# Expert layers: down projection with activations as the stationary operand, residual stream kept in rows of tokens

## What is computed

```python
x = x + tanh(g_xattn[1]) * L1_xattn_ref(ctx, ctx, layernorm(x), ssm_kernel, D, 8)   # long convolution
x = x + tanh(g_ffn[1])  * L1_ffn_ref(layernorm(x), ...)                             # experts
# L1_xattn_ref: kv = k (x) v; y = causal convolution of kv with ssm_kernel, + kv * D; out = sum of y * q
# L1_ffn_ref:
gate = xf @ Wg + bg                       # router, 6 of 8 kept, softmax
h  = silu(xf @ Wgate + bgate) * (xf @ Wup + bup)      # per expert, hidden 256
eo = h @ Wdown + bdown
share = silu(xf @ Ws_up + bs_up) @ Ws_down + bs_down
out = sum_n eo[n] * w[n] + share
```

## Time and profile before

| | before |
|---|---|
| median of three runs | 2029.07 us (2028.69 to 2031.53) |
| profiled execution, its own time | 2031.29 us |
| its span, first to last instruction | 2029.5 us |
| mean granted TensorE clock over the span | 0.975 |
| TensorE matmul busy | 95% of the span |
| VectorE, ScalarE, GpSimd busy | 73%, 51%, 51% |
| start of `experts_block` | at about 659 us |

### The profile page before, as it was taken

How to read it: one execution, slowest core, us unless ns; L and a number is a source line. 1 busy time by engine, 2 the same in 40 slices (tenths; PEclk the granted TensorE clock), 3 DMA queues, 4 the chain that set the end, 5 groups by cost and what they waited for, 6 DMA issues and landing times.

```text
span 2029.5 us, 27663 instructions
## 1 busy us (share of the span) xinstructions
PE 1920.4 (95%) x10020; PEld 1565.7 (77%) x10050; DVE 1484.9 (73%) x2229; ACT 1027.9 (51%) x1468; POOL 1037.0 (51%) x788
## 2 busy tenths in 40 slices
PE   6999769999997669999999999999999999999998
PEld 5888746666653658888888888888888888888886
DVE  5877569888884777867876976876886787687422
ACT  4447547776764435336337427335434633733532
POOL 1110144444430856665666665666565566576554
PEclk9999889999999779999999999999999999999999
DMA  5866415566645113324244233242332423421422
GB/s 196 312 239 230 180 47 136 145 164 172 148 112 131 62 33 129 95 84 147 72 120 131 73 119 107 96 126 79 130 105 87 142 70 112 146 78 63 135 99 68
DMA packets 170115, 249.72 MB, mean 123 GB/s; under 512 B 91356, under 2 KB 92764, under 8 KB 163708
## 3 DMA queue, kind: packets, MB, share of 16 engines
q1 hardware_dynamic: 169692, 247.86, 39.7%
q10 hardware_dynamic: 288, 0.10, 0.0%
HBM read 193.13 MB, written 33.69 MB: 112 GB/s over the span
## 4 chain that ended last, share of the span: by engine, by line
PE 61%; POOL 2%; DVE 1%; issue 1%; DMA 1%; SPq 0%; DVEq 0%; ACT 0%; POOLq 0%; ACTq 0%
PE e_ps_u L54 6%; PE e_ps_out L54 6%; PE e_ps_u L55 6%; PE e_ps_u L56 6%; PE e_ps_out L56 6%; PE e_ps_out L55 6%; PE e_ps_g L55 4%; PE e_ps_g L56 4%; PE e_ps_g L54 4%; PE e_ps_m L56 4%; PE e_ps_m L55 4%; PE e_ps_m L54 4%; PE e_ps_m L2873 1%; DMA e_dn_raw<-in_md 1%; PE e_ps_m L2827 1%
## 5 line engine op out<-in xcount | busy, mean ns | idle before, releaser
L1418 POOL TENSOR_TENSOR e_gu_lo<-e_gu_raw,e_gu_hi 128x1024 fp32r<-128x1024 f32 (+1 forms) x128 | 287.8, 2251 | 176.0 <-ACT e_gu_hi L1722 175.5
L2277 DVE TENSOR_REDUCE e_x3T<-e_zp 128x128 f32<-128x1024 f32 x124 | 256.6, 2070 | 6.4 <-ACT x_held L1837 5.3
L1423 POOL TENSOR_TENSOR e_dn_lo<-e_dn_raw,e_dn_hi 128x512 fp32r<-128x512 f32 x128 | 183.8, 1438 | 110.2 <-ACT e_dn_hi L1728 109.4
L54 PE MATMUL e_ps_u<-e_xn_hi,e_gu_hi 128*128 128x512 f32 x512 | 203.3, 397 | 0.0
L54 PE MATMUL e_ps_out<-e_hd_hi,e_dn_hi 128*128 128x512 f32 x512 | 201.8, 394 | 0.0
L55 PE MATMUL e_ps_u<-e_xn_lo,e_gu_hi 128*128 128x512 f32 x512 | 199.9, 390 | 0.0
L56 PE MATMUL e_ps_u<-e_xn_hi,e_gu_lo 128*128 128x512 f32 x512 | 199.8, 390 | 0.0
L56 PE MATMUL e_ps_out<-e_hd_hi,e_dn_lo 128*128 128x512 f32 x512 | 199.6, 390 | 0.0
L55 PE MATMUL e_ps_out<-e_hd_lo,e_dn_hi 128*128 128x512 f32 x512 | 199.5, 390 | 0.0
L2209 DVE TENSOR_TENSOR e_hd_lo<-gate_held,e_hd_hi 128x512 fp32r<-128x512 f32 x128 | 146.6, 1145 | 70.2 <-ACT e_hd_hi L1752 70.0
L1439 POOL TENSOR_TENSOR e_kv_raw<-e_ke 128x512 f32<-128x512 f32 x128 | 148.2, 1158 | 82.5 <-DVE e_kv_lo L2241 76.9
(11 more groups left out here) (316 smaller groups left out, 5070.3 us busy)
## 6 DMA issues: line engine op xcount, KB each, us to landing
e_gu_raw<-in_mgu SPq DMA_DIRECT2D x96, 512.0 KB, 3.8
e_dn_raw<-in_md SPq DMA_DIRECT2D x128, 256.0 KB, 2.8
e_wb<-wts SPq DMA_DIRECT2D x8, 1536.0 KB, 7.2
c<-in_ctxT SPq DMA_DIRECT2D x8, 1024.0 KB, 7.7
raw_w<-in_w1T SPq DMA_DIRECT2D x8, 1024.0 KB, 4.9
x_held<-in_w2T SPq DMA_DIRECT2D x8, 1024.0 KB, 7.4
gates<-gate_held SPq DMA_DIRECT2D x8, 1024.0 KB, 5.6
vals<-o SPq DMA_DIRECT2D x8, 1024.0 KB, 4.9
```

What stands on the lines that cost most here:

```text
L54: nc.tensor.matmul(out, w_hi, x_hi, start=first, stop=False, skip_group_check=skip)
L1418: nc.gpsimd.tensor_tensor(gu_lo[:, s % 2, a], gu_raw[:, s % 2, a], f32(gu_hi[:, s % 2, a]), ALU.subtract).then_inc(gulo_done, 1)
L1423: nc.gpsimd.tensor_tensor(dn_lo[:, s % 2], dn_raw[:, s % 2], f32(dn_hi[:, s % 2]), ALU.subtract).then_inc(dnlo_done, 1)
L2277: nc.vector.tensor_reduce(x3T[:, lb].rearrange("p (b n) -> p b n", b=B)[:, :, hh * CD:(hh + 1) * CD], zv(5, (1, 8), (21, 8)), AX.X, ALU.ad ...
```

## The change

The operands of the down projection change places: the stationary one is now a block of 128 tokens of `hd_hi` or `hd_lo`, the moving one the 512 columns of the down weights. So `ps_out` has tokens on partitions, like `x`. The matmul with the experts' biases (`bias`) is turned in the same way, and the shared bias becomes a further row of it, with weight one.

- `x2T`, `turn_x2`, `read_x2T`, `y`, `copy_x3` and the scaled bias `gb` go.
- `turn_x3` now turns the bare convolution result. Its wait for `add_x2` becomes a wait for the last `add_terms`; its second group waits for `add_x3(q, 0)` instead of for `norm_nat(q, 0)`.
- `add_x2` becomes `add_x3(q, a)`: two instructions of 1024 columns a tile, which read the turned result from PSUM and add into the rows of `x` in place. They stand ahead of `nat_stats(q, a)`. `nat_stats` and `norm_nat` read those rows from SBUF.
- `finish(g, j)` reads `ps_out` and adds into the same rows, for one block of 128 tokens each. `down_done` counts four times in a tile's last step, so that `finish(g, 0)` can begin when the first bank is done.
- `store` writes four transfers of 256 KB, each after its own `finish`.
- The tiles of `x` rotate over three buffers, `o`, `x_next` (new) and `x_held`. `load_x(q)` waits from the fourth tile on for the stores of tile q-3 and no longer for `norm_x` and `read_x2T`.
- GpSimd sets two more small constants at the start.

```diff
+    xs = [keep["o"], sb("x_next", [P, TJ, D]), keep["x2"]]
...
         def load_x(q):
-            sp.wait_ge(xq_done, START + 4 * q)
-            sp.wait_ge(x2T_done, START + 2 * q)
             sp.wait_ge(keep["x2_out"], START + 16 * TJ * NCH)
+            if q >= len(xs):
+                sp.wait_ge(y_out, START + 16 * TJ * (q - len(xs) + 1))
...
         def store(g):
-            sp.wait_ge(y_done, START + 4 * g + 4)
-            sp.dma_start(dram["out"].rearrange("g (k p) n -> g p k n", p=P)[g], y[:]).then_inc(y_out, 16)
+            for j in range(TJ):
+                sp.wait_ge(y_done, START + TJ * g + j + 1)
+                sp.dma_start(row_block(dram["out"], g, j), rows_of(g)[:, j]).then_inc(y_out, 16)
...
-        def add_x2(q, lb=None):
-            if lb is None:
-                dve.wait_ge(red_done, START + sums(CHD * KT * (q + 1)))
-                dve.wait_ge(x2T_done, START + 2 * (q + 1))
-                rows = slice(0, KT)
...
-            nc.vector.scalar_tensor_tensor(out=x3T[:, rows], in0=x3T[:, rows], scalar=keep["gains"][:, 1:2], in1=x2T[:, rows],
+        def add_x3(q, a):
+
+            dve.wait_ge(nat_filled, 2 * q + a + 1)
+            rows = rows_of(q)[:, 2 * a:2 * a + 2]
+            nc.vector.scalar_tensor_tensor(out=rows, in0=area(q, 1 + a), scalar=keep["gains"][:, 1:2], in1=rows,
                                            op0=ALU.mult, op1=ALU.add).then_inc(x3_done, 1)
...
             n = STEPS * g + s
             pe.wait_ge(hdlo_done, START + n + 1)
             pe.wait_ge(dnlo_done, START + n + 1)
-            for k in range(KT):
-                col = slice(k * P, (k + 1) * P)
-                last = products(nc, ps_out[:, k], dn_hi[:, s % 2, col], dn_lo[:, s % 2, col], hd_hi[:, s % 2], hd_lo[:, s % 2], False,
+            for j in range(TJ):
+                tok = slice(j * P, (j + 1) * P)
+                last = products(nc, ps_out[:, j], hd_hi[:, s % 2, tok], hd_lo[:, s % 2, tok], dn_hi[:, s % 2], dn_lo[:, s % 2], False,
                                 s == STEPS - 1, skip=True)
-            last.then_inc(down_done, 1)
-
-        def turn_x2(q, a):
-            pe.wait_ge(x_in, 16 * TJ * (q + 1))
...
+                if s == STEPS - 1 or j == TJ - 1:
+                    last.then_inc(down_done, 1)
...
         def turn_x3(q, a):
-            pe.wait_ge(x3_done, x3_count(q))
-            if a == 0:
-                pe.wait_ge(prod_done, START + 4 * CHD * KT * (q + 1))
-            elif q > 0:
-                pe.wait_ge(xnat_done, START + 4 * q + 2)
+            pe.wait_ge(red_done, START + sums(CHD * KT * (q + 1)))
+            if q == 0:
+                pe.wait_ge(pool_step, SETUP + 3 * len(SPLIT))
+            elif a == 1:
+                pe.wait_ge(x3_done, START + 2 * q + 1)
```

More of the change, by code:

```diff
@@ L1175, in experts_block @@
     RT = 15
+    SETUP = 4
     def view(t, offset, *dims):
@@ L1210, in toep_slot, with rows_of, downs @@
         return (t_lo if low else t_hi)[:]
-    def x3_count(q):
-        return START + (q + KT if q >= 0 else 0)
+    def rows_of(q):
+        return xs[q % len(xs)]
+    def downs(n):
+        g, s = divmod(max(n, 0), STEPS)
+        return START + (STEPS + TJ - 1) * g + s
     def at(op, c, *which):
@@ L1828, in cut_wT @@
             nc.scalar.activation(wT[:], ps_g[0:WROWS], ACT.Copy).then_inc(wThi_done, 1)
[L1830 to L1839 removed]
+        for s in (silu_done, xq_done, ke_done, qe_done, xnat_done):
             act.sem_inc(s, START)
@@ L1845, in setup @@
             nc.scalar.activation(wr[:, :, 0:8], wr_raw, ACT.Copy).then_inc(setup_hi, 1)
-        read_x2T(0, 0)
         setup()
@@ L1856, in _ @@
         read_q(0, 1)
-        read_x2T(0, 1)
         cut_dn(0, 0)
@@ L1875, in _ @@
         keys(1, 0)
-        copy_x3(0, 0)
-        copy_x3(0, 1)
         cut_kv(1, 0)
-        copy_x3(0, 2)
         cut_dn(0, 1)
@@ L1890, in _ @@
         cut_kv(1, 1)
-        copy_x3(0, 3)
-        read_x2T(1, 0)
         cut_gu(0, 2)
@@ L1895, in _ @@
         silu(0, 1)
-        read_x2T(1, 1)
         cut_hd(0, 1)
@@ L1985, in _ @@
         norm_x(2)
-        read_x2T(2, 0)
         cut_kv(2, 0)
@@ L1992, in _ @@
         read_lgT(1)
-        read_x2T(2, 1)
         cut_dn(1, 1)
@@ L2009, in _ @@
         cut_wT(1)
-        for k in range(4):
-            copy_x3(1, k)
         silu(1, 3)
@@ L2089, in _ @@
             at(norm_x, i + 1)
-            at(read_x2T, i + 1, 0)
             at(cut_kv, i + 1, 0)
@@ L2096, in _ @@
             at(read_lgT, i)
-            at(read_x2T, i + 1, 1)
             at(cut_dn, i, 1)
@@ L2113, in _ @@
             at(cut_wT, i)
-            for k in range(4):
-                at(copy_x3, i, k)
             at(silu, i, 3)
@@ L2410, in _ @@
         add_terms(0, 12)
-        add_x2(0, 0)
         multiply(0, 14)
@@ L2414, in _ @@
         multiply(0, 15)
-        add_x2(0, 1)
-        add_x2(0, 2)
         add_terms(0, 15)
-        add_x2(0, 3)
+        add_x3(0, 0)
         nat_stats(0, 0)
+        add_x3(0, 1)
         nat_stats(0, 1)
@@ L2507, in _ @@
         add_terms(1, 15)
-        add_x2(1)
         cut_hd(0, 12)
         gated(0, 13)
+        add_x3(1, 0)
         nat_stats(1, 0)
@@ L2514, in _ @@
         cut_hd(0, 13)
+        add_x3(1, 1)
         nat_stats(1, 1)
@@ L2607, in _ @@
         add_terms(2, 15)
-        add_x2(2)
+        add_x3(2, 0)
         nat_stats(2, 0)
@@ L2614, in _ @@
         cut_hd(1, 13)
+        add_x3(2, 1)
         nat_stats(2, 1)
@@ L2708, in _ @@
             at(add_terms, i + 1, 15)
-            at(add_x2, i + 1)
+            at(add_x3, i + 1, 0)
             at(nat_stats, i + 1, 0)
@@ L2715, in _ @@
             at(cut_hd, i, 13)
+            at(add_x3, i + 1, 1)
             at(nat_stats, i + 1, 1)
@@ L2775, in bias, with down_first @@
             if g == 0:
-                pe.wait_ge(setup_lo, 3)
+                pe.wait_ge(setup_lo, 2)
                 pe.wait_ge(setup_hi, 2)
             pe.wait_ge(wT_done, START + g + 1)
-            for k in range(KT):
-                last = nc.tensor.matmul(ps_out[:, k], bd[:, k * P:(k + 1) * P], wT[:], start=False, stop=False, skip_group_check=True)
+            for j in range(TJ):
+                last = nc.tensor.matmul(ps_out[:, j], wT[:, j * P:(j + 1) * P], bd[:], start=False, stop=False, skip_group_check=True)
             last.then_inc(bias_done, 1)
-        def down_first(g, k):
-            if k == 0:
+        def down_first(g, j):
+            if j == 0:
                 pe.wait_ge(hdlo_done, START + STEPS * g + 1)
@@ L2914, in _ @@
         up(0, 0)
-        turn_x2(1, 0)
         turn_lg(0)
         up(0, 1)
-        turn_x2(1, 1)
         for k in range(3):
@@ L2986, in _ @@
         down(0, 15)
-        turn_x2(2, 0)
         up(1, 0)
         logits(1)
-        turn_x2(2, 1)
         up(1, 1)
```

125 lines of the change are left out of this document (45 added, 80 removed).

## The result

The changed kernel takes 2034.72 us (median of nine executions, 2033.92 to 2036.29) against 2029.07 us of the kernel before (nine executions of it, 2026.66 to 2031.53). The ratio is 1.0029, with a 95% interval of 1.002 to 1.0038: 5.7 us or 0.3% slower, where 18.1 us faster was predicted. The span of its profiled execution is 2033.3 us, against 2029.5.

What follows compares the result with a forecast made beforehand. TensorE was taken to bound the long stretch, with other engines setting the time at both ends. Savings of 12.2 + 0.9 + 1.0 + 4.0 = 18.1 us from 2029.07 gave 2011.0 us, range 2006 to 2020.

Steps and rivals of the forecast that it cites:

- TensorE bounds the long stretch.: From 757 to 2022 us only TensorE's work sets the end; it is busy 1264.04 of 1265.00 us.
- 12.2 us for 14 groups: Removing `turn_x2`'s groups of eight transposes in the long stretch saves 0.87 us each, 12.2 us in all.
- The exchange of operands costs nothing: Down projection matmuls with weights as the moving operand keep 0.23 us from start to start: 0 us.
- rival 3: The 1536 down matmuls get slower with exchanged operands; at 20 ns each the time is 2041.7 us; chance 0.04.
- 0.9 us for the wait of `turn_x3`: TensorE's one wait, `turn_x3` behind `add_x2` in the long stretch, goes: 0.9 us saved.
- 1.0 us in the first tile: On VectorE's path in the first tile the last statistics come 1.0 us earlier; bounds 0 and 2.3.
- rival 4: Moved idle times in the first tile shift TensorE's granted clock; two 4 us stretches give 2015 us; chance 0.08.
- So the cover holds and I take 0: Where tiles meet, VectorE's two new additions fit within margins of 0.94 and 1.06 us, so TensorE loses 0.
- Rival 1: VectorE becomes the bound where two tiles meet, price up to 6.5 us, giving 2017.5 us; chance 0.10.
- 1.37 us of slack against 1.3: 0: SyncE's queue absorbs three more store issues a tile, 1.3 us, before the next expert weight load: cost 0.
- Its store of 256 KB lands in 2.3 to 2.9 us, as such stores do: At the kernel's end the last, smaller store lands sooner, so the span ends 4.0 us earlier, at 2025.5.
- the upper bound of the groups: Most that removing `turn_x2`'s 14 groups could save on TensorE: the full 1.03 us each, 14.4 us.

Runs made afterwards that it cites:

- experiment 6: Kernel of experiment 3 with the 14 groups of eight transposes put back as dead work that nobody reads: 2024.39 us, ratio 0.9976 to the kernel before.
- experiment 1: Changed kernel with the output laid out tile by tile, so each store is a plain 128x512 piece: 2021.04 us, ratio 0.9955 to the kernel before.
- experiment 11: Kernel of experiment 3 with early `x` loads in twelve 32x512 DMAs and GpSimd waiting for `nat_shift`: 2007.42 us, ratio 0.9883 to the kernel before.
- experiment 7: Changed kernel with output tile by tile, `cut_t` unmoved, GpSimd waiting for `nat_shift` before its subtraction: 2013.0 us, ratio 0.9919 to the kernel before.
- experiment 3: Changed kernel with output tile by tile (plain 128x512 stores) and `cut_t(i+2, 0)` moved behind `gated(i, 14)`: 2012.67 us, ratio 0.9915 to the kernel before.
- experiment 2: Changed kernel with only VectorE's order altered, `cut_t(i+2, 0)` moved behind `gated(i, 14)`: 2025.02 us, ratio 0.9978 to the kernel before.
- experiment 4: Changed kernel with only the last tile's four stores each cut into four 32x512 DMAs, same addresses: 2028.85 us, ratio 0.9991 to the kernel before.

## Why the prediction was wrong

- **TensorE bounds the long stretch.** Right. From the second tile's `logits` on nothing but its work, its waits and its clock moved the time in any run, and putting the work back cost its length (experiment 6).
- **12.2 us for 14 groups.** Right: 1.72 to 1.77 us a tile where no wait interferes (163.35 to 161.63 and 161.58), 0.84 to 0.89 a group by experiment 6.
- **The exchange of operands costs nothing.** Right; rival 3, the only one on the slower side, is out. In a tile the 192 down matmuls take 43.95 us from start to start (44.09 in one tile) instead of 43.96.
- **0.9 us for the wait of `turn_x3`.** Right, it didn't come back. From start to start it was worth 1.1: the one period with it took 164.49 us instead of 163.35.
- **1.0 us in the first tile.** From the first statistics to `logits` 90.6 us instead of 91.3 (659.30 to 749.86; 659.86 to 751.17): 0.75 us. `add_x3` at 1.27 to 1.29 us is as estimated.
- **The clock (rival 4).** Not a cause of the loss, but not nothing: up to 1.9 us between kernels with the same first tile, as experiment 1 says.
- **"So the cover holds and I take 0": the step that failed in the long stretch, about 10.2 us.** The six periods from the second tile's `logits` on take 979.7 us in the changed kernel and 969.5 in experiment 11. The idle times of 0.95 and 0.91 us that were to swallow the two additions were read in the last tile. There is no tile i+2 there and so no `cut_t`; in the five tiles before it `cut_t` stands in that chain, as the order of VectorE shows ahead of the prediction (L2214 between `gated` and `e_hd_lo`), with 2.4 us of idle time. For i = 1 the kernel before has 0.28 us of idle time ahead of `gated(14)`, in the lines above, and none ahead of the second statistics. The same sum there gives 1.28 + 1.28 - 0.28 = 2.28 us of delay against a margin of 1.77: no cover. Measured without the collision, 0.20 us are left with `cut_t` in the chain (experiment 7) and 1.47 without it, against the forecast 1.06. Nor did the working ask what GpSimd does at the new time of VectorE's small instructions: `nat_shift` came to lie beside a 2.4 us subtraction, and lost 2.18 us. Rival 1 named the mechanism, with the stretched rows 5 in its favour, and priced it at up to 6.5 us; it got 0.10.
- **"1.37 us of slack against 1.3: 0" for SyncE's queue: failed by 2.0 us.** The slack was counted in issues, and what came late was a landing. The load of down weights issued at 1908.69, behind the stores of the last tile but one, landed 10.2 us later; with plain stores (experiment 1) it took 5.6. ScalarE stood idle for it, and the cutting of the next expert weights is behind it in its order, until TensorE waited 1.7 us for `gu_lo`:

```profile
1918.89 0.63 ACT L1735 ACTIVATE e_dn_hi<-e_dn_raw 128x512 fp32r<-128x512 f32 x1 [4.29 <-DMA e_dn_raw<-in_md]
```

The issues of the new stores also took 0.54 to 1.98 us instead of 0.43; but one plain store of experiment 1 took 2.24 us at the same place, so the form is not the only reason for a long issue.
- **"Its store of 256 KB lands in 2.3 to 2.9 us, as such stores do": the largest failure.** It was read from line 710, whose stores have the size but not the form: 128x512 there, 4x32x512 here. 13.5 us instead of 3.9, 9.6 us. The profile before had DMAs of the right form, `row_block` under its old name `x2_rows`: the early loads `o<-x`, which flow at about 102 GB/s with 2 tenths of the engines for some 6 us. Window 648 to 660 of the kernel before:

```profile
DMA  9446869999879998222222222222222222221000
```

The sum closes, by the profiles: 18.1 predicted, less 10.2, 2.0 and 9.6, gives 3.7 us slower, and the two spans differ by 3.8. The median says 5.7, because the profiled execution of the kernel before was 2.2 us above its median and that of the changed kernel 0.4 above its own; that is scatter between executions. With the two failures mended, experiment 3 is 17.4 us faster (ratio 0.9915). Its periods still hold the 1.4 us that experiment 11 takes out, so that it comes within 0.7 us of the predicted 18.1 is in part luck.

One slip in the range: the upper bound of the groups was 14.4 us, 2.2 more than 12.2, and the range took 1.4 for it. It decided nothing.

## What to carry to other kernels

Price a DMA by its form, not by its size: look for the row of a transfer whose outermost dimension is the same, and keep 128 partitions outermost, in the layout of the output if need be. Read a margin, and the idle time ahead of it, in every kind of tile that the loop has, and never only in the last, where work for later tiles is missing. And where a change moves VectorE's instructions in time, look which of them have both inputs in SBUF and what GpSimd runs at the new time; even the shortest of them can be held up for the whole length of GpSimd's.

## What the runs showed of the hardware

- DMAs with an outermost size of 2, 4 and 128 moved 51, 102 and 380 GB/s, the first two to the same addresses. At the end of the program one issue on SyncE took 0.52 to 3.27 us for 2x32x512, 0.54 to 0.95 for 4x32x512 and 0.33 to 0.34 for 128x512.
- A load of weights behind four stores of 4x32x512 landed after 10.2 us, behind four plain ones after 5.6.
- A wait of TensorE of 2.7 us was followed by a stretch at a granted clock of 0.50 (experiment 2), one of 1.85 us by a clock of 0.58 from 1922 to 1924 us (experiment 4); behind the 1.7 us of the changed kernel it stayed 1.00.
- The first matmul of 512 columns that starts late takes 0.31 us to its successor instead of 0.23.
- A VectorE instruction on two values a partition lasted 0.16 us alone and 2.35 us when it came 0.06 us behind a GpSimd subtraction of 2.4 us; a wait of 0.27 us on GpSimd gave that back.
- Moving the weights instead of the activations leaves a matmul of 512 columns at 0.229 us from start to start.
